# Reordering the head of a four-layer conditioned residual kernel: mixing products before LoRA products, a scanned sort, pair weights on GpSimd

## What is computed

```python
e = argmax(cond, -1)                                            # layer 0: one expert per batch
x += (silu(x @ Wu[e].T + bu[e]) * (x @ Wg[e].T + bg[e])) @ Wd[e].T + bd[e]      # hidden 256
x += x @ Wbase.T + bbase + 2 * sum_e cond[b, e] * (x @ A[e].T) @ B[e].T         # layer 1: LoRA, rank 16
x += x @ (sum_g cond[b, g] * weight[g] * mask).T + bias                          # layer 2: mixed weight
w = softmax(cond); top 2, normalised                             # layer 3: two experts per batch + shared
x += sum_k w[b, k] * mlp(x, expert[b, k]) + mlp(x, shared)       # gelu(x Wg) * (x Wu) Wd, hidden 512
```

## Time and profile before

| | us |
|---|---|
| runs, median (lowest to highest) | 153.79 (153.7 to 154.18) |
| profiled execution, its own time | 154.21 |
| its span, first to last instruction | 152.2 |
| TensorE busy in the span | 147.4 |
| VectorE, GpSimd, ScalarE busy | 110.0, 93.1, 71.6 |

### The profile page before, as it was taken

How to read it: one execution, slowest core, us unless ns; L and a number is a source line. 1 busy time by engine, 2 the same in 40 slices (tenths; PEclk the granted TensorE clock), 3 DMA queues, 4 the chain that set the end, 5 groups by cost and what they waited for, 6 DMA issues and landing times.

```text
span 152.2 us, 3148 instructions
## 1 busy us (share of the span) xinstructions
PE 147.4 (97%) x1091; PEld 134.0 (88%) x1091; DVE 110.0 (72%) x229; ACT 71.6 (47%) x138; POOL 93.1 (61%) x101
## 2 busy tenths in 40 slices
PE   7999999999999999999999999999999999999992
PEld 2468999999976999899989999999989999999881
DVE  2984666666896686768875868876587886968772
ACT  3666444462374554544454354545425434346640
POOL 1002999999910006939994939995875999880000
PEclk9999999999999999999999999999999999999999
DMA  3999999971653667294297477086448047000052
GB/s 93 395 408 401 413 400 394 424 253 39 243 216 109 179 155 253 48 294 140 57 324 243 146 234 243 5 281 225 187 116 297 5 126 287 6 0 0 0 209 71
DMA packets 13919, 30.15 MB, mean 198 GB/s; under 512 B 1344, under 2 KB 8016, under 8 KB 13776
## 3 DMA queue, kind: packets, MB, share of 16 engines
q1 hardware_dynamic: 13472, 28.76, 54.4%
q10 hardware_dynamic: 432, 1.19, 2.2%
HBM read 24.71 MB, written 1.05 MB: 169 GB/s over the span
## 4 chain that ended last, share of the span: by engine, by line
PE 83%; DVE 7%; ACT 3%; POOL 3%; issue 2%; ACTq 0%; DVEq 0%; POOLq 0%
PE pair L554 21%; PE acc L603 10%; PE pair L544 9%; PE pair L490 9%; PE pair L561 8%; PE acc L588 6%; PE acc L498 5%; PE acc L612 5%; PE acc L445 3%; PE pair L452 2%; PE pair L523 2%; DVE hid L776 2%; DVE hid_lo L767 2%; POOL duo_lo L378 2%; DVE x_hl L741 2%; ACT hid_hi L438 2%
## 5 line engine op out<-in xcount | busy, mean ns | idle before, releaser
L378 POOL TENSOR_TENSOR duo_lo<-raw_duo,duo_hi 128x512 fp32r<-128x512 f32 x36 | 49.1, 1364 | 2.9
L767 DVE TENSOR_TENSOR hid_lo<-hid,hid_hi 128x512 fp32r<-128x512 f32 (+1 forms) x41 | 36.1, 883 | 17.8 <-ACT hid_hi L438 17.3
L438 ACT ACTIVATE hid_hi<-hid 128x512 fp32r<-128x512 f32 (+1 forms) x41 | 25.4, 622 | 44.0 <-DVE hid L776 41.1
L375 POOL CAST duo_hi<-raw_duo 128x512 fp32r<-128x512 f32 x36 | 28.4, 790 | 27.1 <-PE acc L603 27.1
L776 DVE TENSOR_TENSOR hid<-pair,act 128x512 f32<-128x512 f32 (+1 forms) x49 | 32.9, 673 | 5.6 <-PE pair L554 4.1
L554 PE MATMUL pair<-x_duo,duo_hi 128*128 128x256 f32 x192 | 35.1, 281 | 0.2 <-POOL duo_lo L378 0.2
L419 ACT ACTIVATE act<-pair 128x512 f32<-128x512 f32 x48 | 28.3, 590 | 9.6 <-PE pair L554 7.7
L554 PEld LDWEIGHTS pair<-x_duo,duo_hi 128*128 128x128 f32 x192 | 29.6, 188 | 0.9 <-issue 0.4
L554 PE MATMUL pair<-x_duo,duo_lo 128*128 128x256 f32 x96 | 26.8, 279 | 0.0
L544 PE MATMUL pair<-x_hl,shared_hi 128*128 128x512 f32 x64 | 20.5, 402 | 0.0
L554 PEld LDWEIGHTS pair<-x_duo,duo_lo 128*128 128x128 f32 x96 | 18.0, 188 | 0.0
(11 more groups left out here) (101 smaller groups left out, 200.6 us busy)
## 6 DMA issues: line engine op xcount, KB each, us to landing
raw_duo<-experts SPq DMA_DIRECT2D x12, 768.0 KB, 5.1
ring<-experts SPq DMA_DIRECT2D x16, 386.5 KB, 6.5
raw_solo<-experts SPq DMA_DIRECT2D x8, 768.0 KB, 4.7
x_duo<-x_hl SPq DMA_DIRECT2D x24, 128.0 KB, 3.8
x<-xT ACTq DMA_DIRECT2D x1, 1024.0 KB, 6.6
lora_raw<-x SPq DMA_DIRECT2D x4, 256.0 KB, 2.3
raw_solo<-shared SPq DMA_DIRECT2D x1, 768.0 KB, 10.9
out<-lora_raw SPq DMA_DIRECT2D x3, 256.0 KB, 3.1
```

What stands on the lines that cost most here:

```text
L375: pool.tensor_copy(duo_hi[:, j % HALVES, piece(n)], raw_duo[:, j % RAWS, piece(n)])\
L378: pool.tensor_tensor(duo_lo[:, j % HALVES, piece(n)], raw_duo[:, j % RAWS, piece(n)], duo_hi[:, j % HALVES, piece(n)].bitcast(F32), ALU.su ...
L438: act.activation(hid_hi[:, k % SPLITS, at], hid3[:, u % PAIRS, at], ACT.Copy)\
L767: dve.tensor_tensor(hid_lo[:, k % SPLITS, at], hid3[:, u % PAIRS, at], hid_hi[:, k % SPLITS, at].bitcast(F32), ALU.subtract).then_inc(hid_ ...
```

## The change

- Loads: SP issues `cond`, `w2` in two halves with a semaphore each, x, `small`; ScalarE issues `lora`, behind a preload of the exp table. `condT` is gone; DELTA moves from `small` to the front of `w2`, and `cond` carries the transposed weights and an expert pattern (`TURNED`, `OF`).
- A product of `OF` with the spread transposed weights puts the batch weights on all partitions. `y_delta` reads it from PSUM; ScalarE copies `cond_rep` out of it.
- VectorE: `y_delta` comes first, then `at_row`, `onehot`, `chosen_b`; `bs_w` follows the rank copies. The sort has the odd bit of an integer count, one running sum (`tensor_tensor_scan`) and a predicated copy in place of comparisons, masked sums and selects.
- Pair weights, the weight part of the payload and the sum of the payload's two halves are GpSimd's.
- TensorE: the warm products are 3 + 1 short + 1 short + 1 + 1; the mixing products stand before the LoRA products; the payload product is one instead of two, and stands at batch 2 of layer 0 (`SORTED`); the loop waits for the four LoRA copies only.
- ScalarE copies two mixing banks before the LoRA banks and two after the silu of batches 0 and 1.
- GpSimd no longer waits for the slots, multiplies the mask in four large instructions for sixteen, and holds the third piece of duo 1 until two low parts of layer 3 are done.
- SP loads the shared expert ahead of batch 7 and layer 3's first pair behind batch 15.

The diff, cut to its core:

```diff
@@ sync
             sp.dma_start(cond_sb[:, :], cond).then_inc(cond_in, 16)
-            sp.dma_start(lora_sb[:, :], lora).then_inc(lora_in, 16)
-            sp.dma_start(w2_sb[:, :, :], w2).then_inc(w2_in, 16)
+            sp.dma_start(w2_sb[:, 0:W2_HALF], w2[:, 0:W2_HALF]).then_inc(w2_in[0], 16)
+            sp.dma_start(w2_sb[:, W2_HALF:], w2[:, W2_HALF:]).then_inc(w2_in[1], 16)
+            sp.dma_start(x[:, :], xT).then_inc(x_in, 16)
+            sp.dma_start(small_sb[:, :], small).then_inc(small_in, 16)
...
-            for b in range(4, SLOTS0):
-                load0(b)
-            sp.dma_start(shared_sb, shared).then_inc(shared_in, 16)
-            for b in range(SLOTS0, SLOTS0 + 2):
+            for b in range(4, B):
+                if b == SLOTS0 - 3:
+                    sp.dma_start(shared_sb, shared).then_inc(shared_in, 16)
                 load0(b)
             sp.wait_ge(slots_done, 1)
             duo_expert = values(mybir.EngineType.SP, slot_row[0:1, SLOTS:SLOTS + 2 * DUOS], E)
             load_duo(0)
-            for b in range(SLOTS0 + 2, B):
-                load0(b)
             load_duo(1)
@@ gpsimd
+            pool.wait_ge(inv_done, 1)
+            weighed(pool.tensor_scalar(probs[:, :], expd[:, 0:K], inv[:, 0:1], None, ALU.mult))
+            pool.tensor_tensor(pair_sum[:, :], probs[:, 0:1], probs[:, 1:2], ALU.add).then_inc(pair_done, 1)
...
+            pool.wait_ge(placed_done, 1)
+            weighed(pool.tensor_tensor(payload[:, 2, :, :], placed[:, :, :],
+                                       pw_all[:, :].unsqueeze(2).to_broadcast([B, K, SLOTS]), ALU.mult))
+            pool.wait_ge(placed_done, 3)
+            pool.tensor_tensor(payload_sum[:, :, :], payload[:, :, 0, :], payload[:, :, 1, :], ALU.add)\
+                .then_inc(payload_done, 1)
             pool.wait_ge(small_in, 16)
-            pool.wait_ge(slots_done, 1)
...
+            for i in range(MIXES * TILES):
+                n, h = i // TILES, i % TILES
+                pool.wait_ge(mix_copied, i + 1)
...
+                pool.tensor_tensor(dst, mix_raw[:, n, h, :, :, :], mask.unsqueeze(2).to_broadcast([P, KB, B, J]),
+                                   ALU.mult).then_inc(lin2_done, 1)
...
                 for n in range(3):
+                    if j == 1 and n == 2:
+                        pool.wait_ge(hid_lo_done, 2)
@@ scalar
-            act.dma_start(cond_rep[:, :], rep).then_inc(rep_in, 16)
-            act.dma_start(small_sb[:, :], small).then_inc(small_in, 16)
-            act.dma_start(x[:, :], xT).then_inc(x_in, 16)
+            act.preload_act_table(ACT.Exp)
+            act.dma_start(lora_sb[:, :], lora).then_inc(lora_in, 16)
...
+            act.wait_ge(ydelta_done, 1)
+            act.activation(cond_rep[:, :], pair[0][0][:, 0:B * J].rearrange("p (b j) -> p b j", j=J)[:, :, 0],
+                           ACT.Copy).then_inc(rep_done, 1)
             act.preload_act_table(ACT.Silu)
...
+            mixed(0)
+            mixed(1)
             for q in range(G):
                 act.wait_ge(prep_mm, q + 1)
...
+                if b < 2:
+                    mixed(2 + b)
@@ tensor
             pe.wait_ge(zeros_set, 1)
-            warm(5)
+            warm(3)
+            warm(1, P)
+            pe.wait_ge(cond_in, 16)
+            pe.matmul(pair[0][0][:, 0:B * J].rearrange("p (b j) -> p b j", j=J), cond_sb[0:E, OF:OF + P],
+                      cond_sb[0:E, TURNED:TURNED + B].unsqueeze(2).to_broadcast([E, B, J]), start=True, stop=True)\
+              .then_inc(rep_mm, 1)
+            warm(1, P)
             pe.wait_ge(ones_set, 3)
             pe.wait_ge(at_diag_done, 1)
...
-            warm(2)
+            warm(1)
+
+            pe.wait_ge(ydelta_done, 1)
+            for k in range(E):
+                if k % (E // 2) == 0:
+                    pe.wait_ge(w2_in[k // (E // 2)], 16)
...
             for q in range(G):
-                prepare1(q)
...
+                pe.wait_ge(bsw_done, q + 1)
+                if q >= FREE:
+                    pe.wait_ge(mix_copied, q - FREE + 1)
...
             upgate0(0)
-            pe.wait_ge(payload_done, 3)
-            pe.wait_ge(prep_copied, 2 * QUADS + G)
...
+            pe.wait_ge(lora_copied, G)
             for b in range(B):
                 if b + 1 < B:
                     upgate0(b + 1)
-                if b == FREE:
+                if b == SORTED:
+                    pe.wait_ge(payload_done, 1)
+                    pe.wait_ge(mix_copied, 3)
+                    pe.matmul(pair[2][0][:, 0:3 * SLOTS], ones[:, :], payload_sum[:, :, :].rearrange("b v s -> b (v s)"),
+                              start=True, stop=True).then_inc(slots_mm, 1)
+                if b == SORTED + FREE:
                     pe.wait_ge(slots_done, 2)
@@ vector
+            dve.wait_ge(rep_mm, 1)
+            dve.wait_ge(w2_in[0], 16)
+            dve.tensor_tensor(y_delta[:, :, :], pair[0][0][:, 0:B * J].rearrange("p (b j) -> p b j", j=J),
+                              w2_sb[:, 0:J].unsqueeze(1).to_broadcast([P, B, J]), ALU.mult).then_inc(ydelta_done, 1)
             dve.wait_ge(at_mm, 1)
             dve.tensor_copy(at_row[:, :], acc[1][0:1, 0:B]).then_inc(at_done, 1)
+            dve.tensor_tensor(onehot[:, :, :], top_at[:, 0:K].unsqueeze(2).to_broadcast([B, K, E]),
...
+            dve.wait_ge(rank_mm, 1)
+            dve.tensor_copy(count_i[:, :], pair[0][1][0:B, E:2 * E]).then_inc(route, 1)
+            dve.tensor_copy(rank_n[:, :], pair[0][1][0:B, 0:2 * E]).then_inc(rank_done, 1)
+            dve.wait_ge(exp_done, 1)
+            dve.reciprocal(inv[:, 0:1], expsum[:, :]).then_inc(inv_done, 1)
+            dve.wait_ge(rep_done, 1)
             dve.wait_ge(lora_in, 16)
...
+            dve.tensor_scalar(odd_i[:, :], count_i[:, :], 1, None, ALU.bitwise_and).then_inc(route, 1)
...
+            dve.tensor_tensor_scan(starts[:, :], parts[:, 0:2 * E], none[:, :], 0.0, ALU.add, ALU.add).then_inc(route, 1)
...
+            dve.copy_predicated(slot_e[:, :], is_odd[:, :], starts[:, E:2 * E]).then_inc(route, 1)
```

More of the change, by code:

```diff
@@ L45 @@
 PACK3 = 3 * H3
-HALF = P // 2
-J = HALF // E
-QUADS = 2
-RANKED = 12
-BASE1, MASK2, DELTA, BIAS1, BIAS2 = 0, P, 2 * P, 2 * P + J, 2 * P + J + 1
+TILES = 2
+ROWS = P // TILES
+J = ROWS // E
+KB = N // (B * J)
+MIXES = E // KB
+W2_HALF = J + E // 2 * P
+BASE1, MASK2, BIAS1, BIAS2 = 0, P, 2 * P, 2 * P + 1
 SMALL = BIAS2 + 1
@@ L116, with build_kernel @@
 SUMMED = dict(zip(ORDER, itertools.accumulate(additions(unit) for unit in ORDER)))
-def build_kernel(nc, xT, cond, condT, lora, small, w2, experts0, experts3, shared, out):
+def build_kernel(nc, xT, cond, lora, small, w2, experts0, experts3, shared, out):
     ctx = ExitStack()
@@ L432, in _ @@
                     if k >= SPLITS:
-                        act.wait_ge(down_done, [AT[x] for x in SPLIT_AT][k - SPLITS] + 1)
+                        act.wait_ge(down_done, [AT[other] for other in SPLIT_AT][k - SPLITS] + 1)
                     width = N // splits(unit)
@@ L502, in _ @@
             pe.wait_ge(x_in, 16)
-            pe.wait_ge(route, RANKED)
+            pe.wait_ge(rank_done, 1)
             upgate0(0)
-            pe.wait_ge(payload_done, 3)
-            pe.wait_ge(prep_copied, 2 * QUADS + G)
-            for k in range(K):
-                ins = pe.matmul(prep[0][:, 0:3 * SLOTS].rearrange("p (v s) -> p v s", v=3), ones[:, :],
-                                payload[:, :, k, :], start=(k == 0), stop=(k == K - 1))
-            ins.then_inc(slots_mm, 1)
+            pe.wait_ge(lora_copied, G)
             for b in range(B):
@@ L677, in _ @@
-            assert step[0] + 1 == RANKED
-            chained(dve.tensor_copy(rank_n[:, :], pair[0][1][0:B, 0:2 * E]))
-            rank = rank_n[:, 0:E]
-            chained(dve.tensor_tensor(reached[:, :, :], rank_n[:, E:2 * E].unsqueeze(2).to_broadcast([B, E, B]),
-                                      cond_sb[:, EVENS:EVENS + B].unsqueeze(1).to_broadcast([B, E, B]), ALU.is_ge))
-            chained(dve.tensor_reduce(even_odd[:, 0, :], reached[:, :, :], mybir.AxisListType.X, ALU.add))
-            chained(dve.tensor_tensor(even_odd[:, 1, :], rank_n[:, E:2 * E], even_odd[:, 0, :], ALU.subtract))
@@ new lines, in _ @@
+            dve.tensor_tensor(is_odd[:, :], rank_n[:, 0:E], parts[:, 1:E + 1], ALU.is_ge).then_inc(route, 1)
+            dve.wait_ge(route, 8)
+            dve.tensor_tensor(slot_e[:, :], starts[:, 0:E], rank_n[:, 0:E], ALU.add).then_inc(route, 1)
+            dve.wait_ge(route, 10)
+            dve.copy_predicated(slot_e[:, :], is_odd[:, :], starts[:, E:2 * E]).then_inc(route, 1)
+            dve.wait_ge(route, 11)
+            dve.tensor_tensor(slot_ke[:, :, :], onehot[:, :, :], slot_e[:, :].unsqueeze(1).to_broadcast([B, K, E]),
+                              ALU.mult).then_inc(route, 1)
```

214 lines of the change are left out of this document (98 added, 116 removed).

## The result

The changed kernel took 155.32 us (median of nine runs, 154.43 to 155.78); the kernel before, run beside it, 153.70 (153.08 to 155.09). The ratio is 1.0098, with a 95% interval from 1.0069 to 1.0127: slower by 1%, where 0.6% faster was forecast. The profiled execution took 155.65 us, its span 153.9 for 152.2.

A forecast was written before the change was run, and what follows sets the result against it. TensorE, busy 97% of the span, was taken to bound the kernel; 1.0 gained at batch 1's start, less 0.29 for the payload product, plus 0.2 from the hold, gave 0.9 us off: median 152.9, range 151.9 to 153.9.

The forecast's parts named there:

- To 7.1 come 7.3 pairs: Mixing products in the head: 7.3 of 16 pairs run slow until the clock rises at 7.1 us, the rest end at 8.2.
- rival A: Clock rises late, at 10.7 us, through idle time at 4.1 to 4.7: 0.9 us lost, median 154.7; chance 0.1.
- two take 0.29: Payload product at batch 2 of layer 0: two records cost 0.29 us, half of four records' 0.58.
- Gain 0.2: Holding duo 1's last piece keeps GpSimd off VectorE, ending TensorE's 0.22 us wait at 46.28; between 0 and 0.22 us.
- the start of the mixing products: TensorE's head: mixing products start at 5.3 us, where the first LoRA product started at 5.00 before.
- w's half: Load of w's first half (264 KB), issued at 1.2 us, lands 2.8 us later, at 4.0; bounds 3.5 and 5.6.
- ring 7 in time: Ring load 7, behind the shared load in layer 0, lands at 19.9 us, needed at 20.9: cover 1.0 us.
- the batch at 1.34 us: Layer 0's loop: each batch after the payload step still takes 1.34 us on TensorE.
- B: Head: w's half lands no earlier than the whole, at 5.6 us; median 153.6; chance 0.1.
- C: Layer 0: the early shared load delays a ring load past 20.9 us; 1 us later costs 1 us, 153.8; chance 0.06.
- D: Head: clock up a microsecond earlier (0.5), spreading product and w at lower ends (0.3): 152.0; chance 0.1.
- ring 0: First ring load on SP's queue in the head lands at 10.15 us, needed at 11.7.

The follow-up runs named there:

- the versions with both: Changed kernel with `onehot` first, batch weights by transfer with five long warm products, 128-row payload, no hold: 0.9991; the same with x on ScalarE's queue: 0.9994.
- the last version: Changed kernel with `onehot` first, batch weights by transfer, 128-row payload, no hold, and x back on ScalarE's queue: 153.13 us, ratio 0.9994 to the kernel before.
- filled-gap kernel: Changed kernel with extra warm products filling TensorE's idle time before the rank products: 155.10 us, ratio 1.0114 to the kernel before.
- payload early: Changed kernel with the payload product ahead of the loop instead of at batch 2: 154.99 us, ratio 1.0095 to the kernel before.

## Why the prediction was wrong

**The failed step: "To 7.1 come 7.3 pairs"**, the clock's rise taken as a fixed time. It came at 10.2 and 8.4 in the two profiles of the changed kernel, and at 7.6 to 10.2 in all nine that have its head or most of it. That gives 14.11 for 12.6 at batch 1: half of 3.1 us. At the forecast's own rise the structure holds: 14.11 less half of 3.1 is 12.6, and the second profile, 13.22 at 8.4, lies on the same line. So rival A had the mechanism, down to its price of half a microsecond for each. Its place, the idle time, is not confirmed: with it filled the rise was still at 10.0. Its median of 154.7 is near the 154.62 and 155.32 measured in part by luck, since it knew nothing of what the payload product, the hold and the later losses named below cost beyond the forecast, 1.1 us in the first profile. It had a chance of 0.1. The argument against it, that from 5.3 us on TensorE has no gap, was true, and the rise was late all the same.

**A wrong reading behind it.** One rise of one execution was read as the kernel's. The repeated kernel before rose by 4.5, with nearly the same median (153.59). The rows for a mobile rise were not in the first trace; the 0.48 us spread named there was too small a sign, since the kernel before hides an early rise behind its sort. The changed kernel has taken that limit away: the start of its batch 1 follows the level. The Trainium skill, "TensorE: Matmul & The Clock Gate", section "What's actually happening", warns that the number of slow matmuls differs between runs of one kernel. The two profiles of each kernel agree with it (7.1 and by 4.5; 10.2 and 8.4).

**"two take 0.29"**, the payload product: mis-sized. It measured 0.55 us. Half of four records' time took all of it as a cost of each record. But two records alone take 0.39 us to the next start (17.84 to 18.23), and the steps just before and just behind them are 0.1 us longer each than the loop's others: at the change to 16 rows and at the change back a weight load starts only with its product. On 128 rows the step is 0.16.

**"Gain 0.2", the hold:** mis-sized. The wait went, and even 0.38 us with it, and was given back at the third low part, which the held piece met: nothing in sum on the kernel before. The prediction placed the piece right (2 us after the second low part) and asked only who needs it, not whom it hinders.

**Not foreseen:** 0.16 near 65 and some 0.5 us at 110 to 135 in this one profile. From 54 us to the end that is 0.6; of the other eight with the changed head, the one with more warm products loses 0.4 (with the same 0.25 us wait for GpSimd) and the rest 0 to 0.3. Its cause isn't settled. In sums, for the first profile: 1.5 from the rise, 0.3 payload, 0.2 hold, 0.6 late make the 2.6 us between a forecast span 0.9 shorter and one 1.7 longer. For the second profile it is 0.6, 0.3, 0.2 and 0.2, between 0.9 shorter and 0.3 longer.

**Right:** the start of the mixing products (5.50 for 5.3), w's half (4.1 for 4.0), `bs_w` ready before its products, no ScalarE stall, ring 7 in time, the batch at 1.34 us. B, C and D did not occur. Wrong without cost: ring 0 at 10.4 there, but up to 11.7 in its variants, for 10.15, which the slow clock hid; `lora`, forecast to be issued near 2.1 us behind the table load, was issued at 0.8 beside it and landed at 3.0; and D's own terms give 152.1, where 152.0 and 151.9 stand.

**Open:** which part of the head makes the rise late. In the kernel before, fewer full products (with the idle time that they leave) and few-row products in their place each go with a slower kernel. In the changed one no single repair gains beyond the intervals, and the versions with both are level with the kernel before. A gap with no product taken out was not tried, and no variant was profiled twice. Why, and when exactly the level rises, these runs don't say.

## What to carry over

Take a second profile before a clock's rise goes into a sum: a kernel that is fed by something else in its head hides how the rise moves, and removing that limit exposes it. Warm products that look idle are not free to remove: taking two or three out of the kernel before, or giving three of them 8 rows, went with 0.8 to 1.0% more time. A small product between large ones is to be priced with the change to its rows and back; here zeros up to 128 rows gave 0.4 us of it back in the profile. And when a step is held back, ask which instruction it runs beside in its new place.

## What the hardware did that was not expected

- Warm products on 8 rows, as long as the full ones, left the kernel as slow (1.0104) as none at all (1.0076).
- A 16-row product between 128-row ones cost 0.55 us, a 128-row one 0.16. The Trainium skill, "TensorE: Matmul & The Clock Gate", section "Step-by-step: what each phase is for", says that for the time of a weight load the row count doesn't matter: the loads agree (0.29 and 0.30 us for two). When they start is another matter, and there the two kernels differ.
- A 128x512 step on VectorE (`x_hl`) took 0.68 us alone and up to 1.81 beside a GpSimd step on a 128x512 tile; in the repeated kernel before (1.76) and in the last version (1.81), TensorE then waited for VectorE.
- In three profiles TensorE stands still before its first duo product, by 1.11 us in the filled-gap kernel:

```profile
51.14 0.47 PE L591 MATMUL pair<-x_duo,duo_hi 128*128 128x256 f32 x2 [1.11 <-issue]
```

The others are the kernels with more warm products (0.78 us) and with the payload early (0.93). In all three the second gather of `x_duo` landed late, 3.8, 3.4 and 3.6 us after its issue for a median of 2.3, and the product started 0.09 us behind that landing. In all three a 16 KB instruction fetch, starting at 47.8 to 48.5 us, crosses that gather on the DMA engines; in the other profiles of the changed kernel and its variants no such fetch starts between 47 and 49.8, and this gather lands in 2.2. Nothing was changed to test it. That stop is why those spans are long for their level.
